# The causal mask of the attention scores: from matmuls on TensorE to selects on GpSimd

## What is computed

```python
scores = jnp.einsum('bhqd,bhkd->bhqk', Q, K) * (1.0 / jnp.sqrt(jnp.asarray(hs, x.dtype)))
causal = jnp.tril(jnp.ones((T, T), dtype=bool))
scores = jnp.where(causal, scores, jnp.asarray(-10000000000.0, x.dtype))
att = jax.nn.softmax(scores, axis=-1)
y = jnp.einsum('bhqk,bhkd->bhqd', att, V)
```

## Time and profile before

| | |
|---|---|
| median of 3 runs | 415.25 us (414.31 to 416.29) |
| profiled execution: its own time | 415.93 us |
| its span | 414.1 us |
| busy PE / PEld / DVE / ACT / POOL | 354.2 / 163.4 / 286.2 / 257.9 / 110.2 us |
| matmuls `big<-earlier_query,identb` | 176, 37.2 us busy |
| chain that ended last: PE, DVE, ACT, POOL | 58%, 21%, 5%, 2% |
| softmax of batches 0, 1, 2, 3, some marks | 48 to 93, 106 to 134, 197 to 226, 290 to 317 us |

### The profile page before, as it was taken

How to read it: one execution, slowest core, us unless ns; L and a number is a source line. 1 busy time by engine, 2 the same in 40 slices (tenths; PEclk the granted TensorE clock), 3 DMA queues, 4 the chain that set the end, 5 groups by cost and what they waited for, 6 DMA issues and landing times.

```text
span 414.1 us, 7342 instructions
## 1 busy us (share of the span) xinstructions
PE 354.2 (86%) x2700; PEld 163.4 (39%) x2700; DVE 286.2 (69%) x595; ACT 257.9 (62%) x300; POOL 110.2 (27%) x159
## 2 busy tenths in 40 slices
PE   3768688897899699998898899998797898879995
PEld 3424254456454334334454434335453223131122
DVE  4769868897879677774869676874759257953333
ACT  9370443344368778665368688655458797948970
POOL 6245306201703024432503034332400032122000
PEclk9968799999699999999899899999999999989999
DMA  7334214100018155520019155531021256605551
GB/s 269 83 69 70 50 30 68 24 5 0 4 36 99 36 139 140 138 57 9 22 38 102 37 136 132 143 55 28 2 44 33 79 136 168 104 1 135 145 142 39
DMA packets 27116, 31.55 MB, mean 76 GB/s; under 512 B 6780, under 2 KB 17788, under 8 KB 27068
## 3 DMA queue, kind: packets, MB, share of 16 engines
q1 hardware_dynamic: 23372, 28.57, 30.4%
q0 software_dynamic: 3456, 2.39, 3.4%
q10 hardware_dynamic: 252, 0.11, 0.2%
HBM read 3.57 MB, written 1.05 MB: 11 GB/s over the span
## 4 chain that ended last, share of the span: by engine, by line
PE 58%; DVE 21%; issue 6%; DMA 5%; ACT 5%; POOL 2%; SPq 1%; POOLq 0%; DVEq 0%; ACTq 0%
PE misc L1269 20%; PE big L1269 18%; PE acc L1269 17%; DVE mx L1014 7%; ACT ring L752 4%; DMA tstack<-tp 4%; PE misc L1291 2%; DVE xn L955 2%; SPq L516 1%; DMA gm<-wT 1%; POOL block L577 1%; DVE gm L1130 1%; POOL rpow L627 1%; DVE stats L930 1%; DVE tf L1068 1%
## 5 line engine op out<-in xcount | busy, mean ns | idle before, releaser
L752 ACT ACTIVATE ring<-big 128x1024 f32<-128x1024 f32 (+2 forms) x225 | 197.6, 928 | 110.7 <-PE big L1269 109.4
L1014 DVE TENSOR_REDUCE mx<-misc 128x1 f32<-128x320 f32 (+7 forms) x157 | 89.1, 590 | 25.0 <-PE misc L1269 23.0
L1269 PE MATMUL acc<-ring,cb 128*32 128x512 f32 x512 | 67.8, 604 | 2.6 <-DVE gm L1130 1.8
L1269 PE MATMUL big<-tstack,w1s 128*128 128x512 bf16 x192 | 56.4, 388 | 9.6 <-DMA tstack<-tp 4.9
L1269 PE MATMUL big<-dense,block 128*128 128x512 bf16 (+7 forms) x256 | 56.1, 325 | 1.8 <-ACT ring L752 1.2
L1130 DVE SCALAR_TENSOR_TENSOR gm<-acc,cb,gm 128x512 f32<-128x512 f32 (+1 forms) x41 | 30.0, 734 | 27.5 <-DMA gm<-wT 17.4
L1269 PE MATMUL misc<-dense,block 128*128 128x256 bf16 (+7 forms) x174 | 43.4, 312 | 4.2 <-DVE mx L1014 2.9
L1269 PE MATMUL acc<-ring,vals 128*32 128x64 f32 (+7 forms) x512 | 43.4, 438 | 0.4
L1269 PEld LDWEIGHTS big<-dense,block 128*128 128x128 bf16 x256 | 31.1, 150 | 25.5 <-ACT ring L752 11.8
L665 POOL TENSOR_TENSOR gm<-osb,gm 128x512 f32<-128x512 f32 x12 | 15.3, 1272 | 95.0 <-ACT osb L792 62.7
L445 POOL DMA_DIRECT2D block<-qk_turned x66 | 39.3, 600 | 1.5 <-issue 1.4
(11 more groups left out here) (161 smaller groups left out, 452.0 us busy)
## 6 DMA issues: line engine op xcount, KB each, us to landing
gm<-wT SPq DMA_DIRECT2D x64, 256.0 KB
dense<-qk SPq DMA_DIRECT2D x42, 64.0 KB
tstack<-tp SPq DMA_DIRECT2D x18, 128.0 KB, 5.1
block<-qk_turned POOLq DMA_DIRECT2D x66, 32.0 KB, 4.0
xs<-in_x SPq DMA_DIRECT2D x4, 256.0 KB, 8.0
ca<-in_pack_a SPq DMA_DIRECT2D x1, 769.0 KB, 7.2
out<-lg SPq DMA_DIRECT2D x3, 256.0 KB, 2.3
dense<-tp SPq DMA_DIRECT2D x6, 128.0 KB, 8.8
```

Of the source, the lines that this page charges most:

```text
L752: act.activation(dst, src, func, scale=scale).then_inc(s["ring_read"], 1)
L1014: dve.tensor_reduce(mx[:, g, k:k + n, blk], src, AX.X, ALU.max).then_inc(s["misc_read"], 1)
L1269: return pe.matmul(dst, lhsT, rhs, start=start, stop=stop)
```

## The change

The matmuls of `earlier_query` are gone. Instead POOL runs `mask` behind the exponential: for each unit two `affine_select`, one for each half of the partitions, in place in the slot of `ring`; what fails the comparison of query and key position becomes 0. Blocks 0 to 3 have 2 x 64 columns in a select, blocks 4 to 7 have 4 x 64. That is 24 units x 2 = 48 selects a batch, 192 in all. POOL waits for all units of a block to be through ACT, and before each unit for all its own selects so far. `weigh` now waits on `masked`, a count of selects, in place of `ring_read`. The calls of `mask` are put between POOL's other steps.

```diff
+            def mask(m, *blocks):
+
+                phase = softmax_at(m) if m == 0 or m == NB - 1 else softmax_at(None, m - 1)
+                for g, blk in blocks:
+                    units = [u for u in range(NU) if SCORE_UNITS[u][0] == blk]
+                    pool.wait_ge(s["ring_read"], phase[0] + g * NU + units[-1] + 1 + CREDIT["ring_read"])
+                    n, w = GP // len(units), T - BLK * blk
+                    for k, u in enumerate(units):
+                        pool.wait_ge(s["masked"], masked_at(m, g, blk) - 2 * (len(units) - k))
+                        for a in range(2):
+                            keys = ring[BLK * a:BLK * a + BLK, (g * NU + u) % RING, 0:n * w]
+                            keys = keys.rearrange("p (n w) -> p n w", w=w)[:, :, 0:BLK]
+                            ins = pool.affine_select(out=keys, in_=keys, compare_op=ALU.is_ge, fill=0.0, base=0,
+                                                     pattern=[[0, n], [1, BLK]], channel_multiplier=-1)
+                            ins.then_inc(s["masked"], 1)
+                pool.wait_ge(s["masked"], masked_at(m, *blocks[-1]))
...
             stack_q(1)
+            mask(0, (0, 0), (0, 1))
             pool.wait_ge(s["qk_turned"], 6)
             stack_k(1)
-            k_blocks(1, K_BLOCKS)
+            for k in range(6):
+                mask(0, divmod(k + 2, NS))
+                k_blocks(1, K_BLOCKS[2 * k:2 * k + 2])
+            mask(0, (1, 0), (1, 1), (1, 2))
...
             fold_out(0)
             pool.wait_ge(s["xb_ready"], 1)
+            mask(0, *[(1, blk) for blk in range(3, NS)])
...
                 fold_experts(here)
+                pool.wait_ge(s["expert_gates"], 3 * b + 3)
+                mask(b + 1, (0, 0))
                 rsqrt(2 * b + 2, 0)
+                pool.wait_ge(s["pow_ready"], 2 * b + 3)
+                mask(b + 1, (0, 1))
                 rsqrt(2 * b + 3, 1)
+                pool.wait_ge(s["pow_ready"], 2 * b + 4)
+                mask(b + 1, (0, 2), (0, 3))
                 fold_out(b + 1, here)
+                pool.wait_ge(s["xb_ready"], b + 2)
+                mask(b + 1, (0, 4))
                 add_bias(here)
+                pool.wait_ge(s["x1b_ready"], b + 1)
+                mask(b + 1, (0, 5), (0, 6), (0, 7), (1, 0), (1, 1), (1, 2))
                 stack_q(b + 2)
+                mask(b + 1, *[(1, blk) for blk in range(3, NS)])
                 stack_k(b + 2, b)
...
-                        matmul(dst[:, w * j:w * j + w], blocks(k_block_of[m], p, blk), q_dense_of[m][:, p, at:T], start=(j == 0), stop=False)
-                    diagonals = dst.rearrange("p (n w) -> p n w", w=w)[:, :, 0:BLK]
-                    ins = matmul(diagonals, identb[:, :],
-                                 earlier_query[:, :].unsqueeze(1).to_broadcast([P, per, BLK]), start=False)
+                        ins = matmul(dst[:, w * j:w * j + w], blocks(k_block_of[m], p, blk), q_dense_of[m][:, p, at:T],
+                                     start=(j == 0), stop=(j == per - 1))
...
-                pe.wait_ge(s["ring_read"], phase[0] + g * NU + units[-1] + 1 + CREDIT["ring_read"])
+                pe.wait_ge(s["masked"], masked_at(m, g, blk))
```

More of the change, by code:

```diff
@@ L271, in build @@
         later_key = sb("later_key", [P, BLK], BF16)
-        earlier_query = sb("earlier_query", [P, BLK], BF16)
         sil = sb("sil", [P, 3, NB])
@@ L351, in build @@
             "nought_ready", "zeroed", "cleared", "k_block_cleared", "spare_cleared", "mod_linked", "marks", "tabled", "shapes_ready", "exp_ready", "abs_ready", "sil_ready", "mod_ready",
-            "gates_filled", "setup_link", "modb_ready", "w1_ready", "rows_cleared", "tokens_one",
+            "gates_filled", "setup_link", "modb_ready", "w1_ready", "masked", "rows_cleared", "tokens_one",
             "var_ready", "pow_ready", "xn_ready", "out_gates", "expert_gates", "xb_ready", "x1b_ready",
@@ L410, in wait_slot_free, with masked_at @@
                 wait_consumed(eng, phase, CONSUMER[phase[2]][u - RING] - GROUPS[phase[2]])
+        def masked_at(m, g, blk):
+            units = [len([unit for unit in SCORE_UNITS if unit[0] == b]) for b in range(NS)]
+            return 2 * ((NG * m + g) * NU + sum(units[0:blk + 1]))
         def wait_softmax_over(eng, m, turn=None):
@@ L577, in _ @@
             pool.memset(block0[:].rearrange("r p a t -> r (p a t)").bitcast(F32), 0.0).then_inc(s["zeroed"], 1)
-            for t in (later_key, earlier_query, ident, identb):
+            for t in (later_key, ident, identb):
                 pool.memset(t[:, :], 0.0)
@@ L587, in _ @@
                 rows = slice(BLK * h, BLK * h + BLK)
-                pool.wait_ge(s["shapes_ready"], 3 + 2 * h)
+                pool.wait_ge(s["shapes_ready"], 3 + h)
                 pool.affine_select(out=later_key[rows], in_=later_key[rows], compare_op=ALU.is_ge, fill=MASKED,
                                    base=0, pattern=[[-1, BLK]], channel_multiplier=1).then_inc(s["shapes_ready"], 1)
[L593 to L596, removed]
+            pool.wait_ge(s["shapes_ready"], 5)
             pool.wait_ge(s["zeroed"], 1)
@@ L609, in stack_q @@
                 mark()
+                pool.wait_ge(s["marks"], 2 * b + 1)
                 query_blocks(pool, b, Q_BLOCKS[0], "q_block0")
@@ L618, in stack_k @@
                 mark()
+                pool.wait_ge(s["marks"], 2 * b + 2)
             def k_blocks(b, blocks):
@@ L710, in _ @@
             fold_experts(here)
+            pool.wait_ge(s["expert_gates"], 3 * NB - 3)
+            mask(NB - 1, (0, 0), (0, 1))
             rsqrt(2 * NB - 2, 1)
+            pool.wait_ge(s["pow_ready"], 2 * NB - 1)
+            mask(NB - 1, (0, 2), (0, 3))
             fold_out(NB - 1, here)
+            pool.wait_ge(s["xb_ready"], NB)
+            mask(NB - 1, (0, 4))
             add_bias(here)
+            pool.wait_ge(s["x1b_ready"], NB - 1)
+            mask(NB - 1, *[(0, blk) for blk in range(5, NS)], *[(1, blk) for blk in range(NS)])
             experts_out(NB - 2, between={5: lambda: rsqrt(2 * NB - 1, 1)})
@@ L1568, in _ @@
             gates()
-            pe.wait_ge(s["shapes_ready"], 7)
+            pe.wait_ge(s["shapes_ready"], 5)
             ahead = ("second", 0)
```

## The result

The changed kernel takes **445.62 us** (median of 4 runs, 444.20 to 448.15), against 414.84 for the kernel before in the same comparison: **1.0755 times as long, 95% interval 1.0707 to 1.0803**, about 31 us slower. The profiled execution has a span of 443.9, before 414.1. The prediction was 437.0 in a range of 422 to 452: the right sign, a result inside the range, 8.6 us too low.

A forecast was written before the change was run, and what follows sets the result against it. PE was busy 86%, but PE's fixed order, held back by weighings waiting for POOL's selects, was taken to decide. Terms 2 + 9.3 + 7.3 + 4.2 less 1 gave 437.7 profiled, 437.0 us forecast, range 422 to 452.

The forecast's parts named there:

- The size of PE's saving: Mask matmuls taken off PE: 256 times 0.03 us, at most 7.7 us, only where PE isn't waiting for something else.
- The saving counted as nothing where PE waits for POOL: Softmax stages: PE's gain there taken as nothing; -1 left, from `early_scores` (0.7) and a few tenths elsewhere.
- the walk: POOL, ACT and PE timelines followed through the four softmax stages: 2 + 9.3 + 7.3 + 4.2 = 22.8 us later.
- Select prices: POOL's selects of 128 and 256 columns at about 0.31 and 0.47 us, 80 us more POOL busy in all.
- The place that decides: Batch 2, group 1: `stack_q` between selects of blocks 2 and 3; both weighed at 229.15 instead of 223.0; batch +7.3.
- Batch 3: Stage without `stack_q`: `fold_out` and `add_bias` ahead of block 5, then weighings waiting for exponential and select in line: +4.2.
- Batch 0: First softmax stage: selects about 1 to 1.6 late, last weighing waits 1.2 for one more select: +2 (0.5 to 4).
- Experts: Stages of experts: -1, mainly 8 masks a batch off `early_scores`, 0.7 for three batches, plus a few tenths elsewhere.
- Rival A: Contention: selects wait on average 0.3 for DVE's routing, +11 in batches 1 to 3, 448 us; chance 0.17, with dearer selects.
- Rival B: Stalls absorbed: flat-cost selects or better overlapping waits, 429 us; 421 with `stack_q` off the chain too; chance 0.20.
- C: Faster: POOL masks every block before PE comes to it: 412 us, 408 with the last select hidden; chance 0.08.
- D: Costs cancel: time within 0.5% of the kernel before; chance 0.05.

The follow-up runs named there:

- experiment 2: The changed kernel with no selects at all, weighings waiting for the exponential and scores left unmasked: 409.80 us, ratio 0.9872 to the kernel before.
- experiment 5: The changed kernel with the mask matmuls of the kernel before put back beside the selects: 450.39 us, ratio 1.0850 to the kernel before.
- experiment 12: The changed kernel with six of eight 512-column two-SBUF-operand DVE routing operations of batches 0 to 2 cut to an eighth of their columns: 444.15 us, ratio 1.0694.
- experiment 1: The changed kernel with `stack_q` of batches 1 and 2 moved behind all selects of the batch: 434.97 us, ratio 1.0478 to the kernel before.
- experiment 6: The changed kernel with `stack_q`, `fold_out` and `add_bias` all behind the selects of their batch: 429.58 us, ratio 1.0350 to the kernel before.
- experiment 4: The kernel before, with POOL's `fold_out` and `add_bias` waiting until DVE has written `xn`: 409.59 us, ratio 0.9857 to the kernel before.

## Why the prediction was right or wrong

**The size of PE's saving: 7.7 at most; it is 4.8** (experiment 2, where nothing waits for a select). That only 0.03 us separate a mask from the next matmul was the right row to go by, not the 0.19 beside it.

**The saving counted as nothing where PE waits for POOL.** This step put the whole saving at 1, and experiment 5 measures 4.8 for the matmuls in the changed kernel by the medians. By stage the step holds better than the total says: in the three stages with the long waits 1.8 of 5.2 is left. The error is in batch 0, whose sum has no saving although PE waits little for selects there (the matmuls are worth 4.2 in experiment 5, 2.1 in experiment 2). Against the kernel without masks the selects cost 35.8, of which the 22.8 of the walk covers less than two thirds. The forecast missed by 8.6 and not by 13 because the two errors, too small a saving and too small a cost, partly cancel.

**Select prices: right.** 43.5 / 128 = 0.34 and 30.1 / 64 = 0.47, in all 75 us more on POOL, where 0.31, 0.47 and 80 were said.

**The place that decides: right.** Block 2, then `stack_q`, then block 3. With the stage's shift of 13.94 taken off, `stack_q` ends at 227.1 (predicted 227.0), and the weighing of block 3 begins at 229.2. Here the first part of the error enters: I had both weighings through at 229.15; block 3's ends at 230.5. (Up to there the walk is close: the last weighing of group 0 was 1.1 late, where 0.9 was said.) About 0.6 of these 1.3 is the select that waited for DVE (experiment 12), 0.56 the lower clock, 1.30 in place of 0.74. I had priced instructions after a 5 us stall at what they cost without one. From the start of this weighing to the end of the next one (block 4) the low clock costs 1.5 in all, 3.5 in place of experiment 1's 2.0. The last weighing ends at 236.5 (predicted 234.7), the first Gelu comes at 238.6 (236.9). The same holds for batch 1 (+1.85 over the sum).

**Batch 3: +4.2 was 3.4 too small, the worst term.** The waits are there as foretold, but more of them, and with a slow clock:

```profile
340.94 1.29 PE L1313 MATMUL acc<-ring,vals 128*32 128x320 f32 x8 [1.47 <-POOL ring L639]
...
344.88 0.53 PE L1313 MATMUL acc<-ring,vals 128*32 128x192 f32 x8 [0.42 <-POOL ring L639]
...
346.40 0.42 PE L1313 MATMUL acc<-ring,vals 128*32 128x128 f32 x8 [0.62 <-POOL ring L639]
347.50 0.32 PE L1313 MATMUL acc<-ring,vals 128*32 128x64 f32 x8 [0.67 <-POOL ring L639]
```

The granted clock from the stage's first matmul to the first Gelu was 0.79, and 0.94 before the change. In experiment 12 the selects here were shorter and the weighing of 320 columns took 0.75, and the stage was 1.0 shorter to the table load. Experiment 1 has the changed kernel's own order in batch 3, with the clock at 0.87, and was 0.3 shorter. How the 3.4 divide between the waits and the clock is open.

**Batch 0: +2 (0.5 to 4) came out at +2.9**, by small waits at most pairs; the last weighing there waits 0.88 for its select, where 1.2 was said. Experiments 1 and 6, which are the same up to there, have +4.0 and +4.2.

**Experts: -1, measured -0.9, by luck.** The term was mainly the matmuls that `early_scores` loses. Those of batches 2 and 3 stand in the first two stages of experts in the table, which changed by -0.1 and +0.5. The -1.3 that makes the sum lies behind the last softmax, where the kernel before has no mask matmul at all. What made it isn't shown.

**Rival A, contention, was priced at +11; experiment 12 finds about 1.5**, not clear of noise, for most of the operations that A names. The trace now shows the side that was missing: six selects take 3.33 beside the full routing and 2.40 beside the short one. That agrees with the rule of the Trainium skill ("SBUF — State Buffer", Who interferes with whom), by which a GpSimd instruction that reads SBUF and a DVE instruction with two SBUF inputs wait for each other. DVE's `xn` beside POOL's multiplies (2.94 against 1.11, experiment 4) is another case: it has one input tensor, and by the same section it would contend only in a mode that uses both pairs of ports; no run here shows which mode it ran in. A stretched select mostly ends before PE wants it. The number came near A's 448 for other reasons: the clock after a stall, and more small waits than the walk had. That such a result "fits A" without the mechanism being A is why the experiment was needed.

**Rival B's figure for `stack_q` off the chain**, 8 us (429 to 421), measured 10.7 (experiment 1). **C and D** did not happen: the point I gave, a block masked within about 1 us of its exponential, is missed even with nothing but selects in the queue. In batch 2 of experiment 6 (429.58) the last exponential ends at 239.36 and the last select at 240.78, 1.4 later.

## What to carry to other kernels

A step moved to an idle engine is paid for where another engine waits for it, not by the share of the idle engine that it fills: the same selects cost 35.8 us over no selects with PE waiting for them and nothing with nobody waiting. The step's own length counts as part of that latency (half the selects: 21.3 us less). Walk the receiving engine's queue in its order and look for what stands ahead of the moved step at the consumer's turn (here six DMA issues, 10.7 us in two places), count the hand-overs behind the last producer of each batch, and price what runs after a stall of several us at the low clock, as the weighings behind 5.6, 5.0 and 4.1 us of idle time ran here. And look at what the idle engine's present work does to its neighbours before giving it more: two waits that keep POOL's multiplies off DVE's `xn` gave the kernel before 1.4% (interval 1.05 to 1.81), while the change asked about cost 7.5%.

## What the hardware showed that I had not expected

- POOL's multiplies of 512 columns beside DVE's `xn`, which has one input tensor, cost DVE more than twice its time: four instructions took 2.94 and 3.03 us against 1.11 alone. The prediction had looked for contention on the selects and overlooked the one already there.
- After an idle time of 5.64 us on PE the weighing of 320 columns and the 8 score matmuls behind it ran at the lower clock level (granted clock 0.50), 1.30 and 1.28 us; after a wait of 1.29 the same took 0.74 and 0.80 (granted clock 1.00 at the weighing). But experiment 12 shows a weighing mostly at the low clock (1.53) behind a wait of 1.79, where the changed kernel has 0.96 behind the same wait: which waits end in a slow stretch was not foreseeable from the rows.
- Taking all mask matmuls from PE gave 4.8 us by the medians, with waits for selects and without, but in different stages: with the waits, 4.2 of it lie before batch 1's stage and 1.8 in the three stages with long waits, and without them 2.1 and 5.2. The rest of the sums (the stages of experts and the end) is of either sign, up to 1.7 us, and is not explained.
